# First attention: the second block of a batch normalised in the first-tiles part, and its two column halves transposed in two turns of the loop instead of one

## The reference

```
def _L0_xattn_ref(x, context, Wq, Wk, Wv, Wo, bo):      # x is already layer-normed
    h, d = (16, 64)
    q = (x @ Wq).reshape(b, n, h, d).transpose(0, 2, 1, 3)
    k = (context @ Wk).reshape(b, -1, h, d).transpose(0, 2, 1, 3)
    v = (context @ Wv).reshape(b, -1, h, d).transpose(0, 2, 1, 3)
    sim = jnp.einsum('bhid,bhjd->bhij', q, k) * d ** (-0.5)
    attn = jax.nn.softmax(sim, axis=-1)
    out = jnp.einsum('bhij,bhjd->bhid', attn, v)
    return out.transpose(0, 2, 1, 3).reshape(b, n, h * d) @ Wo + bo
...
x = x + _L0_xattn_ref(_layernorm(x, axis=-1), ctx_768, ...)
```

## Time and profile before

| | |
|---|---|
| median of 3 runs | 1540.32 us (1536.5 to 1541.51) |
| the profiled execution, span | 1543.3 us (the page shows no time around it) |
| TensorE busy | 1304.0 us, 84% |
| VectorE busy | 863.9 us, 56% |
| ScalarE busy | 577.9 us, 37% |
| GpSimd busy | 390.0 us, 25% |
| first attention, its four batches | about 36 to 438 us of the span |

### The profile page before, as it was taken

The page is one execution under the profiler, slowest core; times in us unless marked ns, Lnnn a source line. Parts: engine busy times, 40 slices in busy tenths (PEclk is TensorE's granted clock), DMA queues, the critical chain, the costliest instruction groups (busy, mean ns, idle before and its releaser), DMA issues. The chain is left out here.

```text
span 1543.3 us, 21512 instructions
## 1 busy us (share of the span) xinstructions
PE 1304.0 (84%) x7714; PEld 1160.9 (75%) x7714; DVE 863.9 (56%) x1796; ACT 577.9 (37%) x1362; POOL 390.0 (25%) x356
## 2 busy tenths in 40 slices
PE   5889888897956999999999999975798888878725
PEld 4788787887855888888888888864587877778623
DVE  5467676676634343444434344336446777786578
ACT  4455554555522233232323323221233343434243
POOL 2222232222300222222222222231112332242113
PEclk9699999999977999999999999985567787877655
DMA  6000000000061020303103020310000000000002
GB/s 214 1 1 1 1 0 0 0 0 0 1 160 54 29 83 1 82 0 82 55 27 82 0 83 1 83 40 12 0 1 1 1 1 1 0 0 0 1 18 95
DMA packets 26298, 46.75 MB, mean 30 GB/s; under 512 B 1230, under 2 KB 11198, under 8 KB 26238
## 3 DMA queue, kind: packets, MB, share of 16 engines
q1 hardware_dynamic: 26238, 45.97, 10.2%
HBM read 41.64 MB, written 4.33 MB: 30 GB/s over the span
## 5 line engine op out<-in xcount | busy, mean ns | idle before, releaser
L1032 DVE TENSOR_TENSOR hid<-py,gated 128x512 f32<-128x512 f32 x120 | 82.9, 691 | 291.3 <-POOL gated L978 259.5
L954 ACT ACTIVATE gated<-pg 128x512 f32<-128x512 f32 x120 | 71.7, 598 | 362.4 <-PE pg L915 362.4
L926 PEld LDWEIGHTS acc<-w2T,hidT 128*128 128x128 f32 x1440 | 188.3, 192 | 17.1 <-DVE hidT L1041 7.6
L978 POOL TENSOR_TENSOR gated<-gated,weight_all 128x512 f32<-128x512 f32 x96 | 124.1, 1293 | 299.0 <-ACT gated L954 298.0
L1430 PEld LDWEIGHTS acc<-vbd,probT 128*128 128x128 f32 (+1 forms) x960 | 154.5, 246 | 57.4 <-issue 32.2
L926 PE MATMUL acc<-w2T,hidT 128*128 128x256 f32 x1440 | 193.8, 285 | 2.5 <-DVE hidT L1041 2.2
L915 PE MATMUL py<-xnT,w1T 128*128 128x512 f32 x720 | 191.3, 401 | 0.0
L915 PE MATMUL pg<-xnT,w1T 128*128 128x512 f32 x720 | 186.9, 395 | 0.0
L1430 PE MATMUL acc<-vbd,probT 128*128 (+4 forms) x960 | 155.1, 311 | 37.0 <-DVE probT L1572 36.2
L915 PEld LDWEIGHTS pg<-xnT,w1T 128*128 128x128 f32 x720 | 135.9, 189 | 32.0
L915 PEld LDWEIGHTS py<-xnT,w1T 128*128 128x128 f32 x720 | 128.6, 191 | 21.7
(11 more groups left out here) (235 smaller groups left out, 1972.1 us busy)
## 6 DMA issues: line engine op xcount, KB each, us to landing
weight_all<-weight_rows SPq DMA_DIRECT2D x16, 1024.0 KB, 9.4
weight_all<-weight_rows SPq DMA_DIRECT2D x16, 512.0 KB, 9.5
x_res<-in_x SPq DMA_DIRECT2D x1, 4096.0 KB, 17.4
out<-x_res SPq DMA_DIRECT2D x8, 512.0 KB, 2.6
w1s<-in_L_ffn_W SPq DMA_DIRECT2D x4, 512.0 KB, 8.5
w2s<-in_L_ffn_W SPq DMA_DIRECT2D x2, 768.0 KB, 12.0
wqs<-in_L_xattn_Wq SPq DMA_DIRECT2D x1, 1024.0 KB, 10.8
wos<-in_L_xattn_Wo SPq DMA_DIRECT2D x1, 1024.0 KB, 13.2
```

Of the source, the lines that this page charges most:

```text
L926: last = pe.matmul(acc[j // 2][:, (j % 2) * D:(j % 2 + 1) * D], hidT[c % 3][i][:, j * P:(j + 1) * P], g["w2T"][k][:, c, :], start=(c == 0 ...
L954: act.activation(gated[bank][:, :], pg[bank][:, :], ACT.Silu).then_inc(s["silu_done"], 1)
L978: gp.tensor_tensor(gated[bank][:, :], gated[bank][:, :], weight_all[:, c - SHARED, :], ALU.mult).then_inc(s["silu_weighted"], 1)
L1032: dve.tensor_tensor(hid[c % 3][:, :], py[bank][:, :], gated[bank][:, :], ALU.mult).then_inc(s["hid_done"], 1)
```

## The change

It moves work, and adds or removes none. The normalisation of block 1 (`norm_of(b, 1)`) moves on VectorE from the end of turn 0 into the first-tiles part, between tile 1's last maxima and the sums of its banks 1 and 2. The transposes of column half 0 move to the end of turn 0, and those of half 1 stay at the end of turn 1, with ScalarE's and VectorE's splits in the same turns. VectorE's split of half 1 now stands ahead of that turn's sums. The table `TR_BATCH` follows.

```diff
 TR_BATCH = [use for t in range(1, TILES) for use in
-            [("p", t, gr) for gr in range(len(TR_GROUPS))] + ([("x", 1, dc) for dc in range(DC)] if t == 2 else [])] + TR_BEGIN
+            [("p", t, gr) for gr in range(len(TR_GROUPS))] + ([("x", 1, t - 1)] if t <= DC else [])] + TR_BEGIN
...
(ScalarE)
                 def batch(b, nxt):
                     for t in range(TILES - 2):
                         step(b, t + 1, b, t + 2)
-                        if t == 1:
-                            for dc in range(DC):
-                                split_x(b, 1, dc)
+                        if t < DC:
+                            split_x(b, 1, t)
...
(VectorE)
                     stats_of(b, 1)
                     step(b, 0, b, 1)
+                    norm_of(b, 1)
                     sums(b, 1, range(1, NB))
...
                     for t in range(TILES - 2):
                         step(b, t + 1, b, t + 2)
-                        if t == 1:
-                            split_x(b, 1, 0)
+                        if t < DC:
+                            split_x(b, 1, t)
                         sums(b, t + 2, range(1, NB))
                         add_out(b, t)
-                        if t == 0:
-                            norm_of(b, 1)
-                        if t == 1:
-                            split_x(b, 1, 1)
...
(TensorE)
                         step(b, t + 1, b, t + 2, lambda k: outputs(b, t, range(*OUT_PARTS[k])))
-                        if t == 1:
-                            for dc in range(DC):
-                                transpose_x(b, 1, dc)
+                        if t < DC:
+                            transpose_x(b, 1, t)
```

## The result

Six runs of the changed kernel have a median of 1569.37 us (1566.77 to 1578.02), six of the kernel before 1540.91 us (1536.5 to 1545.37). The ratio is 1.0199, with a 95% interval of 1.0166 to 1.0232: slower by 28.5 us between the medians, where +25.6 us and 1566 were forecast.

The account below looks back on a forecast made before the run. TensorE was taken as the busiest engine, time being lost where it stands still or runs at lower clock. Terms 5.8 + 13.1 - 2.8 + 9.5 = +25.6 us on 1540.3 gave 1566 us, range 1555 to 1573.

Parts of the forecast that it names:

- A: Before turn 0: normalisation ahead of tile 1's sums delays them 1.44 us per batch; +5.8 us over four.
- B: End of turn 0: half 0's trip delays turn 1 by 3.28 us per batch; +13.1 us over four.
- C: Turn 1: with one half and no normalisation it takes 12.03 us instead of 12.72; -2.8 us over four batches.
- D: TensorE's clock: low behind three pauses per batch, seven more low stretches at 1.36 us each; +9.5 us.
- Rival 1: TensorE's clock falls no more often than before the change; +16.1 us, 1556 us; chance 0.14.
- rival 3: End of turn 0: half 0's trip is covered on VectorE, so not slower; -1.0 us, 1539 us; chance 0.04.
- rival 2: TensorE's low-clock stretches last twice as long; +35 us, 1575 us; chance 0.07.

Follow-up runs that it names:

- e1: The kernel before with only block 1's normalisation moved ahead of tile 1's second and third sums; 1553.75 us, ratio 1.0067.
- e2: The changed kernel with the normalisation one place later on VectorE, behind tile 1's sums; 1562.85 us, ratio 1.0125.
- e5: The changed kernel with unused products filling TensorE's pauses, 19 behind the first-tiles part and 14 behind each half; 1567.99 us, ratio 1.0157.
- e3: The changed kernel with VectorE's sums of banks 1 and 2 ahead of the half's split in turns 0 and 1; 1540.97 us, ratio 0.9997.
- e7: The changed kernel with fewer unused products in TensorE's pauses, 10 behind the first-tiles part and 7 behind each half; 1557.25 us, ratio 1.0067.
- e6: e4 with the half's four transposes inside turns 0 and 1's last product group, after three of seven chunks; 1523.58 us, ratio 0.9865.
- e4: The changed kernel with both VectorE edits, normalisation behind tile 1's sums and sums ahead of the half's split; 1538.80 us, ratio 0.9966.

## Why the prediction was right

**A** (+5.8 forecast): 5.3 us, 47.3 - 42.0, and e1 shows the same pause alone. A batch gives 1.28 us and not 1.44, except the first, 1.46: VectorE's neighbours overlap by 0.07 to 0.09 us on either side (178.15 against 177.77 + 0.47, 179.60 against 178.15 + 1.52), and I had laid them end to end. The four instructions took 1.81 us in e2, beside a GpSimd product, and 1.38 alone. The Trainium skill, GPSIMD Engine Reference (Specifications), states such a contention for SBUF; the trace agrees, with 1.81 against 1.38.

**B** (+13.1): 13.2 us, read from e5. The 3.88 us taken from turn 1 of before came out as 3.89. e3 shows that VectorE's order was the reason, as argued: with the sums first the same trip leaves 1.41 us of pause.

**C** (-2.8): -2.8 us, read from e5.

**D** (+9.5): 11.1 us. Turns 0 and 1 are 108.6 us together after the change and 96.3 in e5, 12.3 more, and 1.25 of these before had too. This term was mis-sized by 1.6 us. The count of seven was right, but its ground was not. I had written that a pause of 2.9 us lies near the point where the clock falls, and that the three pauses are longer. Length alone doesn't decide: e7's clock fell behind 1.82 us, e2's stayed up behind 3.21, and in e1 turn 1's two pauses of before, 1.41 and 1.7, were followed by a full turn 2 in two batches of four. That all twelve stretches came is in part luck, and what decides is open. A stretch costs 1.47 and not 1.36, and in the first batch the clock fell inside the pause before turn 0 and stayed low for 6.8 us, until 83.1, which cost turn 0 2.07 instead of 1.25. The 0.84 us that I read from turns 2 and 3 of the second batch was wrong: e1, e3 and e5 have turn 2 at full clock, 8.76 us, so it lost 1.48 like the others. The diagonals lengthen turns 3 and 4, and not turn 2 as I took it. Only the mean without that row entered the sum, so the error went into the third rival's price alone (5.9 given back, not 4.0).

5.3 + 13.2 - 2.8 + 11.1 = 26.8 us, the difference in the table. A's 0.5 too much and D's 1.6 too little cancel in part. The remaining 1.7 of the measured 28.5 between the medians is less than the second attention's spread between profiles. That each batch repeats the last to within 0.1 us was not so in the first, whose turn 0 took 10.00 us before and 14.13 after; the prediction used this difference itself in part D.

Rival 1 (no further falls of the clock, 1556) and rival 3 (the trip covered, 1539) fell with rows of the changed kernel; rival 2 (stretches twice as long) came true in length in one pause of twelve, and cost 0.6 us there instead of the 1.36 that it was priced at, since 2.1 us of that stretch passed while TensorE stood still. The argument for rival 1, a pause of 2.93 us that left the clock up, was weaker than it looked: the same pause let it fall in one batch of four before, in four of four in e2 and in e6, and in three of four in e4. The condition of rival 3 is what e6 builds: half 0's transposes early enough, and VectorE's sums not behind the split.

## What to carry to other kernels

Before a transposed piece is moved to the end of another stage, ask which engine's list it stands in, and in front of what: here the split in front of the sums cost 1.9 us each time, and exchanging the two lines took back the whole loss. A trip through other engines is best started a few products before the end of a run of products, and not behind it (e6: 0.18 us of pause instead of 3.29). Price a pause on TensorE with the slower work that may follow it, here 1.47 us on top of 3.3, and don't take a pause as harmless because it once was. Look at the rest of the program behind a remedy too: e5 took back 18.3 us of the turns and lost 19 in a loop that nobody had edited.

## What the runs showed of the hardware

A pause of 2.9 us on TensorE, with the same work of TensorE around it, was followed by a lower clock in some batches and not in others: one in four before, four in four in e2 and in e6, three in four in e4. The low stretch took 1.25 or 1.48 us from the same turn, and 2.1 to 2.7 where the clock fell inside the pause and stayed low for longer (6.8 us in after, 76.3 to 83.1, and in e4, 171.9 to 178.7). Half filled, with 1.7 to 2.4 us left, pauses were still followed by a lower clock in eight of twelve cases (e7). Pauses of 1.41 to 1.50 us with products before and behind them left it at full in all sixteen cases of e3 and e4. What decides in the other cases is not shown.

e5's profile (21888 instructions against 21512) has 19 more packets of instructions than the eight others, and two stops of TensorE of 6.5 us in a loop that was not edited, each in a transfer of weights and each ended just behind such a packet. With 21704 instructions (e7) there were neither.
